# Expert tiles begun from the counts of eight token tiles, the rest of the router placed between them

## The chip, the cores and the metric

One NeuronCore of a Trainium2 chip runs the kernel. The metric is the device time of one execution in microseconds (us), as the median of several runs. Five engines work side by side, each with an instruction queue of its own: TensorE (PE in the profile, its weight loads PEld), VectorE (DVE), ScalarE (ACT), GpSimd (POOL) and SyncE (SP), which here issues nearly all DMAs. They wait for each other on semaphores. A lower time is better.

## The reference, cut to what matters

A small vision tower: 32 images of 36 patches, 192 channels, that is 1152 tokens. Patch embedding and a three-step "diffuser" attention come first; then a transformer block whose second half is a mixture of 8 experts with 2 chosen for each token:

```python
x = x + _attention(_layer_norm(x, ln1_g, ln1_b), ...)        # 12 heads of 16
xn = _layer_norm(x, ln2_g, ln2_b).reshape(B * N, C)
logits = xn @ gate_w                                          # 8 experts
top_logits, top_idx = jax.lax.top_k(logits, 2)
gates = softmax(top_logits)                                   # at top_idx, else 0
h = gelu(einsum('td,edh->teh', xn, w1) + b1)                  # hidden 768
y = einsum('teh,ehd->ted', h, w2) + b2
x = x + einsum('ted,te->td', y, gates)
```

and a last layer norm of the sum. Inputs have fixed shapes; which expert a token goes to depends on the data.

## The kernel before

**Tiling.** Tokens are worked on in NT = 11 tiles of T = 108 (three images); the last holds 72. The order of attention is `ATT` = tiles 8, 9, 10, 0 to 7, so an index `a` from 0 to 10 counts places in that order. The diffuser's steps come first, then a loop over `i` that runs attention for the tile `i` and, staggered behind it, later steps for the tiles `i - 1`, `i - 2` and `i - 3`: softmax and mixing of heads and projection for `i - 1` (L625 to 714), layer norm and transpose for the router for `i - 2` (L701), logits, choice of two experts, ranks and destination for `i - 3`. The loop runs to NT + 4 (L615, L1217, L1410), so its last iterations hold only the staggered steps of the last tiles. Each engine has this order written out by hand in its own block; within an engine it is strict.

**Router.** `logits(a)` (L586) is a matmul with the gate. `choose(a)` (L1189, VectorE) takes the best two of 8 and makes a 0/1 matrix `chosen`. `ranks(a)` (L593) are two matmuls with triangular and full ones, which give each row's rank within its tile and the tile's total for each expert. `send_to(a)` (L1205) adds the totals so far, `taken`, and gives each row two destinations. `send(a)` (L1402, GpSimd) writes the rows there with two indirect DMAs: `srt_dram` holds, for each expert, a region of rows in order of arrival.

**Table.** When all tiles are counted, VectorE works out the table of expert tiles (L1268 to L1299): the counts are rounded up to tiles of P = 128 rows, NTILE = 25 at most; for each tile its expert (packed seven to an integer, `packs`, semaphore `exp_ready`), the first row of it (`row_i`, `place_ready`), how many rows are valid, and then the softmax gates of all tokens, with an exponential on ScalarE (L988).

**Expert tiles.** SP waits for the table, reads expert and row into registers and loads the tile's `w1` weights (`expert_weights`, L370, three buffers) and its rows (`sorted_rows`, L378, a ring of 8). TensorE transposes the rows (`columns_of`, L724), ScalarE applies gain and bias (L990), VectorE casts to a high half `xh`, GpSimd subtracts to a low part `xl`; `first(i)` (L732) multiplies with `w1` in three terms, ScalarE applies gelu (L1000 to L1004), VectorE casts the hidden values to a high half and subtracts to a low part (`split`, L1305), and `second(i - 1)` (L749) multiplies with `w2`. VectorE adds `b2` (L1339), and GpSimd scatters the rows to `y_dram` (L1440). GpSimd also makes one of 22 diagonal gate matrices a tile (L1435). Some buffers of the tiles lie on those of earlier stages: the third `w1` buffer on the attention's weights, the rows' ring on the attention's buffers. At the end the two results of each token are loaded, weighted and added, and normalised.

## Time and profile before

| | |
|---|---|
| median of 3 runs | 416.79 us (415.52 to 416.88) |
| profiled execution, whole time | 420.47 us |
| its span, first to last instruction | 418.7 us |
| TensorE busy | 368.3 us (88%) |
| VectorE busy | 243.0 us (58%) |
| GpSimd busy | 216.7 us (52%) |
| ScalarE busy | 203.4 us (49%) |
| mean granted TensorE clock | 0.936 of full |

The profile is of one execution. All points in time below are us from the start of its span. Its page cuts the span into 40 slices of 10.5 us; further views group the work by stretch of time, list it in order of time, or follow the chain of work that ended last back from the end. A group's idle time before it, in square brackets, names who released it. The profiled execution's time is 3.7 us over the median of the runs.

In this trace the attention iteration `i` = 10, the last with attention scores, begins at 257.76, and the first expert matmul runs at 295.17.

### The profile page before, as it was taken

Reading aid. Unit: us, or ns where it says so; the run is one execution under the profiler, and the core shown is the slowest. Engines: PE = TensorE matmul, PEld = TensorE weight load, DVE = VectorE, ACT = ScalarE, POOL = GpSimd, SP = SyncE. Lnnn points to the kernel's source line nnn. Section 1 sums busy time; section 2 is a strip of 40 time slices with the busy share of each in tenths; the row PEclk is TensorE's granted clock in tenths of the full one; section 3 lists DMA queues with packets and bytes.
Section 4 is the critical chain, followed back from the end, with each engine's and each line's share of the span. In section 5 each row is a group of like instructions: output and inputs, shape, how many; then the busy total and the mean of one; then the engine's idle time right before and its main releaser. Section 6 shows DMA issues by size and latency. Waiting matters only on the chain.

```text
span 418.7 us, 11108 instructions
## 1 busy us (share of the span) xinstructions
PE 368.3 (88%) x3714; PEld 315.0 (75%) x3714; DVE 243.0 (58%) x721; ACT 203.4 (49%) x519; POOL 216.7 (52%) x361
## 2 busy tenths in 40 slices
PE   4999978999999988999989999760899999999963
PEld 3888745766766756898988999750899999899953
DVE  2111462454654565577876566546489888888622
ACT  1222276777577753657655455320554454454203
POOL 2001168666777652355777455452356667666324
PEclk9999999999999998999997799855699999999988
DMA  8999457966427422100000000024677666675052
GB/s 251 386 386 298 130 178 174 238 144 148 89 43 161 98 33 34 25 1 2 18 19 11 18 18 18 25 65 163 256 267 266 225 252 241 235 258 211 6 176 79
DMA packets 59558, 59.08 MB, mean 141 GB/s; under 512 B 36939, under 2 KB 46197, under 8 KB 58736
## 3 DMA queue, kind: packets, MB, share of 16 engines
q1 hardware_dynamic: 57248, 54.81, 43.1%
q0 software_dynamic: 2256, 3.57, 2.7%
q8 instruction: 32, 0.52, 0.5%
q14 instruction: 22, 0.18, 0.1%
HBM read 25.11 MB, written 14.33 MB: 94 GB/s over the span
## 4 chain that ended last, share of the span: by engine, by line
PE 77%; DVE 9%; issue 5%; ACT 3%; DMA 2%; POOL 2%; SPq 1%; ACTq 0%; POOLq 0%; DVEq 0%
PE bank L414 37%; PE wide L414 33%; PE bank L419 4%; PE bank L729 1%; DMA xT<-in_xT 1%; DVE xT L1160 1%; DVE stats L1037 1%; PE bank L632 1%; POOL rstd L1368 1%; DVE xs L1123 1%; ACT xT L966 1%; DMA xT<-y_dram 1%; ACT xT L800 1%; DMA y_dram<-ysb,ydst 0%; DMA xT<-srt_dram 0%
## 5 line engine op out<-in xcount | busy, mean ns | idle before, releaser
L1440 POOL DMA_INDIRECT y_dram<-ysb,ydst x25 | 25.8, 1032 | 36.1 <-DVE ydst L1321 27.5
L1367 POOL TENSOR_SCALAR veps<-mv 108x1 f32<-108x1 f32 x46 | 10.4, 225 | 61.1 <-DVE mv L1039 59.5
L414 PE MATMUL wide<-w2h,xs 128*128 x300 | 39.1, 246 | 0.0
L414 PE MATMUL bank<-wqv,xTs 128*108 128x384 f32 x96 | 37.4, 514 | 1.1 <-DVE xT L1160 1.0
L414 PE MATMUL wide<-w2l,xs 128*128 x150 | 36.9, 246 | 0.0
L1315 DVE TENSOR_TENSOR xs<-xT,xs 128x384 bf16<-128x384 f32 x50 | 35.6, 711 | 1.7
L831 ACT ACTIVATE xT<-bank,gains 96x128 f32<-96x128 f32 x50 | 20.0, 448 | 32.5 <-PE bank L729 32.5
L1313 DVE CAST xs<-xT 128x384 f16<-128x384 f32 x50 | 28.7, 575 | 11.2 <-ACT xT L1004 10.3
L800 ACT ACTIVATE xT<-bank 108x192 f32<-108x192 f32 (+3 forms) x57 | 20.9, 367 | 29.4 <-PE bank L414 16.2
L414 PE MATMUL bank<-tokw,xT 128*108 128x192 f32 x132 | 27.3, 364 | 6.2 <-DMA xT<-in_xT 5.2
L414 PE MATMUL wide<-xT 64*108 64x36 f32 (+2 forms) x368 | 30.7, 273 | 1.9 <-DVE chosen L1203 1.4
L414 PEld LDWEIGHTS wide<-xT 64*108 64x108 f32 (+1 forms) x368 | 28.3, 175 | 4.0 <-issue 3.6
L414 PEld LDWEIGHTS bank<-tokw,xT 128*108 128x108 f32 x132 | 24.2, 196 | 7.2 <-DMA tokw<-in_tokw 5.2
L414 PE MATMUL bank<-xTs,wqk 128*128 128x108 f32 x176 | 26.6, 297 | 3.2 <-DVE xT L1171 1.9
L1368 POOL TENSOR_TENSOR rstd<-veps,nhalf 108x1 f32<-108x1 f32 x46 | 26.2, 570 | 3.8
L1427 POOL TENSOR_TENSOR xl<-xT,xh 96x256 bf16<-96x256 f32 x25 | 21.0, 839 | 13.3 <-DVE xh L1303 12.7
L414 PEld LDWEIGHTS bank<-xT 108*32 108x32 f32 (+2 forms) x316 | 13.3, 119 | 18.0 <-issue 17.2
L1407 POOL DMA_INDIRECT srt_dram<-row,dst x22 | 23.0, 1044 | 7.1 <-issue 6.0
L414 PEld LDWEIGHTS bank<-xTs,wqk 128*128 128x128 f32 x176 | 23.1, 204 | 4.4 <-ACT xTs L831 2.2
L414 PEld LDWEIGHTS wide<-w2h,xs 128*128 128x128 f16 (+1 forms) x300 | 26.4, 98 | 0.0
L1131 DVE TENSOR_TENSOR rm<-bank,pairm 96x192 f32<-96x192 f32 x24 | 8.5, 353 | 30.8 <-PE bank L414 30.7
L1389 POOL TENSOR_SCALAR nrm<-nrm 108x4 f32<-108x4 f32 (+1 forms) x3 | 0.8, 274 | 47.3 <-DVE nrm L1094 33.0
(241 smaller groups left out, 1089.9 us busy)
## 6 DMA issues: line engine op xcount, KB each, us to landing
srt_dram<-row SPq DMA_DIRECT2D x8, 800.2 KB, 15.3
xT<-in_xT SPq DMA_DIRECT2D x11, 324.0 KB
tokw<-w1h SPq DMA_DIRECT2D x9, 384.0 KB
e1T<-w1l SPq DMA_DIRECT2D x9, 384.0 KB
xT<-in_w SPq DMA_DIRECT2D x8, 384.0 KB, 3.5
hT<-in_w SPq DMA_DIRECT2D x8, 384.0 KB, 3.3
vecs<-w1h SPq DMA_DIRECT2D x8, 384.0 KB
wqv<-w1l SPq DMA_DIRECT2D x8, 384.0 KB
```

The costliest lines, as they stand in the source:

```text
L414: return nc.tensor.matmul(o, l, r, start=start, stop=stop)
L419: last = nc.tensor.transpose(o[:, f, :], i[:, f * HF:(f + 1) * HF], ident[0:T, 0:T])
L800: return nc.scalar.activation(o, i, ACT.Copy)
L831: last = nc.scalar.activation(o[:, f], i[:, f], ACT.Identity, scale=gains[:, which, 0, f:f + 1], bias=gains[:, which, 1, f:f + 1])
L1131: V.tensor_tensor(rm[0:HF, q % 2], bank[3][0:HF, 0:2 * JB * PAIR].rearrange("p (u j c) -> p u j c", u=2, j=JB), pairm[0:HF, None, None, :] ...
L1313: V.tensor_copy(high, hidf[:, i % 2, cols]).then_inc(S["hidh_ready"], 1)
L1315: V.tensor_tensor(hidl[:, i % 2, o].rearrange("p j n -> p (j n)"), hidf[:, i % 2, cols], high, ALU.subtract).then_inc(S["hidl_ready"], 1)
L1367: link(G.tensor_scalar(ve, var, EPS, None, ALU.add))
L1368: last = G.tensor_tensor(rstd[0:rows, k], ve, nhalf[0:rows], ALU.pow)
L1407: G.indirect_dma_start(srt_dram, bass.IndirectOffsetOnAxis(dst[:, t, k:k + 1], 0), row[:, t, 0:W], None, bounds_check=EXP * CAP - 1, oob_i ...
L1427: G.tensor_tensor(xl[0:HF, i % 2], x32[:, i % 2], xh[0:HF, i % 2], ALU.subtract).then_inc(S["xl_ready"], 1)
L1440: G.indirect_dma_start(y_dram, bass.IndirectOffsetOnAxis(ydst[:, q:q + 1], 0), ysb[:, q % YB], None, bounds_check=2 * NTOK - 1, oob_is_err ...
```

## The change

The number of tokens that eight of the eleven token tiles bring (`SOON` = 8, the tiles `a` = 0 to 7, 828 tokens) guarantees that at least `FULL` = 5 expert tiles can be filled with 128 valid rows, whatever the router chooses. The change makes the table twice: a first one of 5 full tiles, with counts rounded down, in VectorE's iteration 10, ahead of the residual of tile 9; and a second one, of the other 20 tiles, after the last tile is counted, which is now in iteration 2 of the expert tiles. SP starts the first tiles from the first table and the stored rows of eight token tiles (`row_stored`), and waits for the second table (`exp_ready` 2, `place_ready` 2, `row_stored2`) before tile 5.

The router's steps move. Within an attention iteration the transpose for the router stands ahead of the values, its columns and the logits follow in the same iteration `i` for the tile `i - 2`; choice, ranks, destination and stores of the tile `i - 3` come at the start of the next. The loop ends at NT. What is left of the last tiles is written out around and between the first expert tiles: on TensorE the last probabilities, mixing, `columns_of(0)`, the last head columns, a router transpose, ranks, the last projection, `columns_of(1)`, `first(0)`, logits; then in tile 1 a transpose, ranks, and logits behind `second(0)`, and in tile 2 the last ranks.

Further edits: ring of 4 rows for 8; the router's columns are double-buffered instead of kept; `b2` is loaded earlier; the third weights' buffer waits for the last projection; for tiles below 5 the high cast of the hidden values is done by ScalarE instead of VectorE and no validity is looked up; the gelu table is loaded by a dummy activation ahead of tile 0; the gates' exponential comes after tile 5's gelus, and the gate diagonals in tiles 7 to 17, two a tile.

```diff
-RING, YB = 8, 3
+RING, YB = 4, 3
+SOON = NT - 3
+FULL = (2 * sum(min(T, B * N - t * T) for t in ATT[:SOON]) - EXP * (P - 1)) // P
+NPACK = 1 + -(-(NTILE - FULL) // PACK)
...
# SyncE
-            sp.wait_ge(S["row_stored"], 16 * 2 * NT)
+            sp.wait_ge(S["row_stored"], 16 * 2 * SOON)
...
             for i in range(WB, NTILE):
+                if i == FULL:
+                    sp.wait_ge(S["exp_ready"], 2)
+                    expert_weights(i)
+                    sp.wait_ge(S["place_ready"], 2)
+                    sp.wait_ge(S["row_stored2"], 16 * 2 * (NT - SOON))
                 sorted_rows(i)
-                expert_weights(i)
+                if i != FULL:
+                    expert_weights(i)
...
# TensorE, behind the attention loop (now range(NT))
+            probabilities(NT - 1)
+            mixed(NT - 1)
+            pe.wait_ge(S["taken_ready"], SOON)
             columns_of(0)
+            head_columns(NT - 1)
+            pe.wait_ge(S["xn_ready"], NT - 1)
+            turn(halves(3), row[:, ATT[NT - 2], 0:C]).then_inc(S["xnT_psum"], 1)
+            pe.wait_ge(S["e_ready"], NT)
+            ranks(NT - 3)
+            projected(NT - 1)
+            columns_of(1)
             pe.wait_ge(S["exp_ready"], 1)
...
+            first(0)
+            logits(NT - 2)
+            for i in range(1, NTILE + 1):
...
+                if i == 1:
+                    pe.wait_ge(S["xn_ready"], NT)
+                    pe.wait_ge(S["srtT_ready"], 2)
+                    turn(halves(1), row[:, ATT[NT - 1], 0:C]).then_inc(S["xnT_psum"], 1)
+                    ranks(NT - 2)
+                if i == 2:
+                    ranks(NT - 1)
+                    pe.wait_ge(S["taken_ready"], NT)
+                second(i - 1, e[(i - 1) % 2])
+                if i == 1:
+                    pe.wait_ge(S["taken_ready"], NT - 1)
+                    logits(NT - 1)
...
# ScalarE, expert tiles
+            nc.scalar.activation(vv[:, 1, 0:1], rowm[:, 0:1], ACT.Gelu)
...
+                gelus(i, (0, 2))
+                if i < FULL:
+                    high_of(i, 0)
+                if i == 1:
+                    router_columns(NT - 1, bank[1][0:HF, 0:2 * T].rearrange("p (f t) -> p f t", f=2))
+                gelus(i, (4,))
+                if i < FULL:
+                    high_of(i, 1)
+                if i == 0:
+                    router_rows(NT - 1)
+                if i == 5:
+                    act.wait_ge(S["gex_in"], 1)
+                    nc.scalar.activation(vv[:, 1, :], vv[:, 0, :], ACT.Exp).then_inc(S["gex_ready"], 1)
...
# VectorE, attention loop
+                if i == SOON + 2:
+                    table_tiles(0, FULL, eoff, 0)
+                    table_experts(0, FULL)
+                    table_places(0, FULL, eoff)
...
+                if i >= 1:
+                    residual(i - 1)
...
# VectorE, expert tiles
+            heads_of(NT - 1)
+            choose(NT - 3)
             sorted_high(0)
+            send_to(NT - 3)
+            residual(NT - 1)
             for i in range(NTILE + 1):
...
+                if i == 2:
+                    send_to(NT - 1)
                 if i < NTILE:
...
+                    if i == 0:
+                        choose(NT - 2)
+                    split(i, 0)
+                    if i == 1:
+                        send_to(NT - 2)
+                    split(i, 1)
...
+                if i == 1:
+                    choose(NT - 1)
+                if i == 2:
+                    table_tiles(FULL, NTILE, start[:], P - 1)
+                    sorted_high(4)
+                    table_experts(FULL, NTILE)
+                    table_places(FULL, NTILE, start[:])
+                if i == 3:
+                    table_valid(FULL, NTILE, start[:])
...
# GpSimd
+            sorted_low(0)
+            sorted_low(1)
+            residual(NT - 1)
+            send(NT - 3)
+            for i in range(1, NTILE + 1):
...
+                if i <= 2:
+                    send(NT - 3 + i)
+                if i == 7:
+                    pool.wait_ge(S["gates_ready"], 1)
```

`table_tiles`, `table_experts`, `table_places` and `table_valid` hold the instructions of L1269 to L1294, each over its own range of tiles and counted from a given start; `high_of` is the cast of L1313 as a ScalarE copy.

## Rows read from the trace of the kernel before

**Rows 1.** The page's 40 equal slices, busy tenths of TensorE and its granted clock.
```profile
PE   4999978999999988999989999760899999999963
PEclk9999999999999998999997799855699999999988
```
**Rows 2.** Stretches: length, busy time (and count) by engine, clock, DMA share, GB/s.
```profile
249.30:257.76 8.46, 8.40 (x85) 7.94 (x85) 5.58 (x21) 4.40 (x13) 3.74 (x6) 1.00 0.07 21
...
265.96:281.20 15.24, 9.79 (x57) 8.87 (x56) 8.27 (x42) 3.68 (x9) 8.14 (x13) 0.62 0.10 27
281.20:291.95 10.75, 0.93 (x4) 0.86 (x5) 6.68 (x31) 0.21 (x1) 3.40 (x4) 0.50 0.52 182
291.95:311.24 19.29, 17.16 (x210) 16.02 (x210) 11.21 (x30) 9.77 (x23) 7.50 (x10) 0.78 0.69 247
311.24:350.00 38.76, 37.77 (x554) 35.79 (x552) 33.53 (x80) 19.38 (x50) 25.59 (x30) 1.00 0.70 250
```
**Rows 3.** Chain that ended last, from residual to first expert matmul: start, us, what.
```profile
274.53 0.37 DVE xT L1260
...
286.00 0.30 DVE packs L1286
...
289.84 1.98 DMA xT<-srt_dram
291.95 0.65 PE bank L729 x2
...
295.17 2.72 PE bank L414 x24
```
**Rows 4.** Short stretches around changes of the granted clock, columns as rows 2.
```profile
225.00:225.50 0.50, 0.50 (x7) 0.50 (x6) 0.47 (x2) 0.18 (x1) 0.50 (x1) 0.68 0.17 47
235.00:235.50 0.50, 0.50 (x4) 0.47 (x2) 0.00 (x0) 0.50 (x2) 0.00 (x0) 0.58 0.14 37
269.00:270.00 1.00, 0.00 (x0) 0.00 (x0) 0.93 (x4) 0.00 (x0) 0.77 (x1) 0.78 0.00 0
300.00:301.00 1.00, 1.00 (x19) 1.00 (x17) 0.95 (x4) 0.75 (x3) 0.14 (x1) 0.86 0.41 160
```
**Rows 5.** Timeline of the attention's end: start, us, engine, line, out<-in, [idle before <-releaser].
```profile
264.28 0.61 DVE L1246 TENSOR_TENSOR xT<-wide,nmax 108x432 f32<-108x432 f32 x1
...
267.36 1.23 PE L414 MATMUL wide<-xT 108*108 108x147 f32 x8 [0.36 <-ACT xT L800]
...
269.49 0.76 DVE L1237 TENSOR_TENSOR xT<-wide,precm 108x576 f32<-108x576 f32 x1
270.30 2.13 PE L414 MATMUL bank<-amask,xT 108*96 108x36 f32 x12 [1.71 <-DVE xT L1237]
...
272.88 1.62 PE L414 MATMUL wide<-wvo,xT 128*108 128x192 f32 x4
274.28 0.83 PE L414 MATMUL wide<-chosen,rank 108*108 108x8 f32 x4
```
**Rows 6.** Timeline of VectorE: last choice, first to last; last placing; the table's first.
```profile
279.99 0.17 DVE L1197 MAX8 best<-wide 108x8 f32<-108x8 f32 x1 [0.33 <-PE wide L414]
...
280.89 0.17 DVE L1203 TENSOR_TENSOR chosen<-mm 108x8 f32<-108x8 f32 x1
...
282.17 0.17 DVE L1209 TENSOR_TENSOR pos<-wide,taken 108x8 f32<-108x8 f32 x1 [1.11 <-PE wide L414]
...
282.93 0.16 DVE L1269 SCALAR_TENSOR_TENSOR tiles_i<-taken,route 128x8 int32<-128x8 f32 x1
```
**Rows 7.** Chain again: the transposes of tiles 5 and 6's rows.
```profile
311.24 0.22 PE bank L729 x2
...
315.13 0.22 PE bank L729 x2
```
**Rows 8.** Timeline of ScalarE: the table load ahead of the first gelu.
```profile
295.06 1.28 ACT L1004 ACT_TABLE_LOAD   x1
```
**Rows 9.** Waits from 198 to 250: who for whom, us in total, times, longest.
```profile
PE wide L414 <- DVE chosen L1203: 1.4, 3, 0.6
```

## What the change does to the time: the prediction

> **What bounds the kernel now.** I read the busy slices of the page first. TensorE is 9 tenths busy or more in nearly every slice, with one hole: slices 26 to 28, where it falls to 6, 0 and 8 tenths while the granted clock reads 5, 5 and 6 tenths [rows 1]. The table of stretches puts times to it. The last full attention iteration (249.30 to 257.76, 8.46 us) has TensorE busy for 8.40 us. After the last iteration's own work (265.96) come 15.24 us with 9.79 busy at a mean clock of 0.62, then 10.75 us with 0.93 busy, then 19.29 us for the first five expert tiles with a mean clock of 0.78; from 311.24 on TensorE is busy 37.77 of 38.76 us [rows 2]. The chain of waits says what fills the hole: residual of the last token tile (274.53), router, counts, the table's experts on VectorE (286.00, 0.30 us, so published at 286.30), the sorted rows' load (289.84, 1.98 us), the transpose of the rows (291.95), and the first expert matmul at 295.17 [rows 3]. So from 265.96 to 295.17, 29.2 us, TensorE does little but a serial tail, and the last 9 us of it start from the finished table. That hole is what the change goes for; the expert tiles behind it are TensorE-bound at 3.89 us each (transposes at 311.24 and 315.13) [rows 7].
>
> The clock matters here. It fell to its lower level (half, 1.2 GHz) within 269 to 270 after TensorE had idled from 268.6, and came back within 300 to 301, some 5 us after matmuls ran densely again. It also fell within 225.0 to 225.5 with thin gaps before it and came back only within 235.0 to 235.5 although TensorE was busy all the time: 10 us [rows 4]. So after a restart I count 5 to 10 us at half clock.
>
> **First table, made early.** Eight token tiles' counts are ready in iteration 10, behind the scores' subtraction of that iteration (264.28 + 0.61 = 264.9) [rows 5]. Before, the table's first instruction started at 282.93 and the experts were out at 286.30, 3.4 us with 25 tiles a row [rows 3, 6]; with 5 tiles its wide instructions shrink, which I put at 0.8 us in all (0 to 1.2): experts at 267.5, places 0.8 us later, the new counts' start 0.4 us more: 268.7. From published experts to the first transpose took 291.95 - 286.30 = 5.65 us on SP and the DMA queue; the same steps give 273.1. The rows of the eighth tile must be stored by then: two indirect DMAs, given their addresses at about 262, have until the load is issued at 271, 9 us, where before the last two had from 283.0 to 289.84, 6.8 us [rows 3, 6].
>
> The cost is a delay behind it: VectorE adds the residual of token tile 9 at 268.7 instead of 266.0, so the last tile's heads (1.0 us for residual and moments, then 1.3) are done at about 271.1 instead of 270.25 (269.49 + 0.76) [rows 5]. On TensorE the last head columns are now queued behind the transpose of the expert rows, so they start at 273.7, not 270.30. TensorE idles from 268.6 (end of the matmuls of 267.36 in [rows 5]) to 273.1, so it restarts at half clock. In order: transpose 0.6, head columns 2.13, row transpose 0.6, ranks 0.83, projection 1.62, second expert transpose 0.6, all at half clock rates [rows 3, 5], sum 6.4: first expert matmul at 279.5. Before it was 295.17. **Tiles begin 15.7 us earlier.**
>
> **Router steps inside tiles 0 to 2.** Choosing takes 1.07 us (279.99 to 281.06) and placing 0.86 us (282.17 to 283.03) on VectorE, pauses included [rows 6]. The chain to the second table: tile 0's first product 3.9 us at half clock (the 2.72 us of 24 matmuls in [rows 3] scaled to 36) to 283.4; logits of token tile 9 0.9; its choice 1.1 (285.3), with tile 0's splitting behind it, 1.2 (286.6). Tile 1's first product (2.0) is over by then; a transpose and ranks 0.6, tile 0's second product 1.5: 288.6; logits of tile 10 0.5. VectorE meanwhile does split, placing of tile 9, split, bias, and then the last choice, over at 290.6. Tile 2's first product ends at 291.2, ranks 0.4, placing 0.9: 292.6. VectorE must still split tile 2 (1.5) and add tile 1's bias (0.4, after the second product at 293.5): 294.5. Then six table instructions for 20 tiles 1.5, a cast 0.3, six more 1.5: **second experts at 297.8**. Add the same 5.65 us: the transpose of tile 5's rows at **303.5**. TensorE is ready for it at about 297.3 and has the first product of tile 4 and the second of tile 3 queued behind it, so it idles about 6 us. In the kernel before this transpose is at 311.24 [rows 7]. So of 15.7 us won, 7.7 are left at tile 5: the second table's chain takes the hole over.
>
> After such an idle stretch the clock will be at half again for at least 5 us, in which some 2.5 us of work is lost, all behind 311.24's counterpart (before, that loss lies ahead of it, in the first tiles). Left: 5.2 us. If the clock comes back 5 us after 273.1 and not 10, the work of 278 to 283 is faster, and the chain ends 2.4 us sooner: 7.6 us. I take the middle, **6.4 us**.
>
> **Other edits.** (a) Expert weights: tile 2's wait for the last projection (278.9), needed by 289; 10 us of cover. (b) A ring of 4 rows for 8: the weights' loads between them already wait for the tile three back, so nothing. (c) The high cast on ScalarE for five tiles, ten casts of about 0.5 us: ScalarE is busy 19.38 of 38.76 us in steady tiles, VectorE 33.53 [rows 2]; this pays for about half of VectorE's 11 us of choosing, placing and table. VectorE's whole work from 268.7 to the fifth bias is some 26.5 us, until 295.2, under 303.5, so it is no bound of its own. (d) Diagonals moved to tiles 7 and on, two at a time: GpSimd busy 25.59 of 38.76 with one of them, about 0.7 us more per 3.9 us tile, still under. (e) The gates' exponential now sits between two gelus. The trace shows one table load, 1.28 us [rows 8]; two of them and the exponential's 0.2 give 2.8 us, against 1.9 us a tile in which ScalarE is free [rows 2, 7]: between 0 and 0.9 us for TensorE, taken as 0, since the products read the gelus a tile later. The same function's table for the first tile is now loaded ahead of the tiles, a gain that lies in the tail's cover.
> (f) Attention iterations: the choice leaves the path of the scores, where TensorE waited for it three times, 1.4 us in all [rows 9]; against this the head columns' copy stands behind the router columns on ScalarE (0.75 us) where TensorE already waits for it, and GpSimd issues the stores, some 2.4 us, ahead of its roots. Bounds: 2 us won (the three gaps and their echo), 2 us lost (0.75 in two or three iterations); taken as 0.
>
> The Trainium skill, "ScalarE: Activation LUTs", section "What ACT_TABLE_LOAD costs", speaks against (e): it adds a drain of some 1.38 us to each switch of tables. In the trace the load of 295.06 follows directly on the activation that ended at 295.04, with no drain to be seen. By that page the two switches would be an estimated 2.8 us dearer, so ScalarE would be 3.7 us late at tile 6 instead of 0.9, and the result up to 2.8 us later: 413.2.
>
> **Sum.** Span 418.7 - 6.4 = 412.3 us; the profiled execution took 420.47, 1.8 around the span: 414.1. The median of the runs shown, 416.79, is 3.7 under that execution; the half clock of 225 to 235 costs 5 us and may be missing in them, so I claim nothing for its going. 416.79 - 6.4 = **410.4 us**.
>
> **Rivals.**
> A. *The second table's wait is small.* If the clock stays up in the tail or comes back at once, and the load overlaps more, what is left is 15.7 less the added work on TensorE (about 2) and the waits between choice and ranks (about 1): up to 13, down to 9: 403.8 to 407.8. For: chains here are of small steps, and TensorE's are the halvable ones. Against: VectorE's steps and the 5.65 us of loading don't shrink. Chance 0.22, at 406.
> B. *The hole moves whole.* VectorE's queue in tiles 0 to 2 holds the last placing back by 3 to 6 us more (a cast beside GpSimd's work, its value loads, GpSimd's stores before the second load): 413.4 to 416.6. Chance 0.18, at 415.
> C. *Slower: the clock stays at half through tiles 0 to 4.* The 10 us of [rows 4] show that busy is not enough. Then two first and two second products in the chain take 7.0 us more, the transpose of tile 5 comes at 310.5, and with 2.5 us at half clock behind it the sum is -1.8: 418.6. It decides from a transpose of tile 5 later than 308.7. Chance 0.09.
> D. *It does not do what it says:* the early load waits for the stores of rows or for the weights' room until the tail is over, so tile 0 isn't early. The added router work remains: 417.5. Chance 0.04.
> Forecast as above, 408 to 413: chance 0.47.
>
> **How the numbers follow.** Range 403.8 (end of A) to 416.6 (end of B), leaving C, D and a strip beyond A. A difference under 0.3%, 1.25 us, can't be told from none here: faster is below 415.5. That is the forecast, A and three quarters of B, 0.82; same is the rest of B and a part of D, 0.06; slower C and most of D, 0.12.
>
> **What would show it.** Right: the first transpose of expert rows near 273, the first expert product near 279.5, a TensorE gap of about 6 us before tile 5's transpose near 303.5, clock at half around both, the same 3.89 us tiles and the same end. Wrong: no gap before tile 5 (A); a first table later than 270; attention iterations longer than 8.5 us late in the stage; the clock never at full between 270 and 303 (C).

## The result

The change doesn't make the kernel faster. In the first measurement the median of 20 runs was 423.75 us beside 422.24 for 20 runs of before. The recorded ratio is 1.0131 [1.0094, 1.0168]; it is that of the fast runs alone, 421.84 in the mean of twelve of the changed kernel over 416.40 in the mean of the first three of before, where the two medians above are only 0.4% apart. Timed twice more beside other kernels, it came out at 0.9993 [0.9936, 1.0050] and 0.9999 [0.9939, 1.0059]. So it is between 1.3% slower and equal; compared at the same mean clock (last section) it is 1.0% slower. The forecast, 410.4 us, 1.5% faster, is excluded by all three, and 423.75 lies outside the range.

The profiled execution took 421.68 us, with a span of 419.9 (before: 418.7). The slices of its page, TensorE and its granted clock, to be compared with [rows 1]:

```profile
PE   4999968999999987999988999797688999999873
PEclk9999999999999999977999989859889999999968
```

The slice in which TensorE stood still is gone; shallow ones took its place (7 tenths in slices 26 and 28, 6 in slice 29). The clock is down in slices 18 and 19, in the attention stage, earlier than before. Stretches of the same execution, columns as [rows 2]: last attention iteration, from there to the first transpose of expert rows, the tail up to the first expert products, tiles 0 to 4, tile 5, the next nine.

```profile
248.47:259.11 10.64, 10.07 (x85) 9.46 (x85) 5.72 (x21) 4.45 (x12) 3.75 (x6) 0.84 0.06 18
259.11:273.77 14.66, 10.74 (x94) 9.84 (x95) 11.58 (x50) 4.87 (x12) 5.42 (x10) 0.84 0.20 72
273.77:279.30 5.53, 5.53 (x30) 5.28 (x31) 1.60 (x8) 3.56 (x8) 0.67 (x1) 0.50 0.53 183
279.30:306.49 27.19, 18.98 (x221) 17.69 (x219) 15.20 (x65) 12.37 (x31) 13.81 (x17) 0.87 0.45 158
306.49:311.87 5.38, 5.38 (x56) 5.37 (x57) 1.22 (x4) 3.00 (x7) 0.66 (x1) 0.68 0.52 183
311.87:346.00 34.13, 31.73 (x469) 30.37 (x467) 28.15 (x70) 18.64 (x45) 22.65 (x28) 1.00 0.67 242
```

And the chain of work that ended last (start, us, what), to be compared with [rows 3, 7]:

```profile
263.47 0.76 DVE xT L1369
270.49 0.68 SPq L392
271.66 1.98 DMA xT<-srt_dram
273.77 0.63 PE bank L757 x2
...
279.10 2.56 PE bank L433 x24
...
292.31 1.97 another core or an unknown queue
295.00 2.02 PE wide L433 x18
303.20 0.67 SPq L392
304.38 2.06 DMA xT<-srt_dram
306.96 2.56 PE bank L433 x24
```

The first rows' load and transpose come 18 us earlier than in [rows 3] (273.77 for 291.95), and a second load, of tile 5's rows, now stands in the chain (304.38). Its transpose at 306.49 is the counterpart of 311.24 in [rows 7].

Stage by stage, from the timelines. A is the start of attention iteration 1 to that of iteration 10, B from there to the first transpose of expert rows, C from that to tile 5's, D from tile 5's to tile 10's, E from tile 10's to the end of the span, all in us:

| kernel | A | B | C | D | E | span |
|---|---|---|---|---|---|---|
| before | 85.4 | 34.2 | 19.1 | 19.5 | 88.1 | 418.7 |
| after | 90.5 | 14.7 | 32.7 | 22.6 | 90.8 | 419.9 |
| after, third time | 84.4 | 14.7 | 32.2 | 24.1 | 89.9 | 415.7 |
| old placing | 84.1 | 16.0 | 32.5 | 23.7 | 89.4 | 416.7 |
| high cast on VectorE | 91.2 | 14.7 | 31.9 | 22.5 | 89.3 | 422.7 |
| gates on GpSimd | 88.4 | 14.4 | 32.0 | 21.2 | 89.8 | 417.1 |
| old placing, short tail | 84.7 | 16.5 | 23.7 | 20.8 | 89.6 | 406.0 |
| the same, gates on GpSimd | 84.4 | 16.3 | 25.0 | 19.6 | 88.1 | 404.3 |

(The kernels below the third line are the experiments. C and D are cut at the first matmul of tile 5's transpose, for before 311.1, not the 311.24 of [rows 7].) In the first pair, B and C together win 19.5 - 13.6 = 5.9 us, and A loses 5.1, D 3.1 and E 2.7. That is 5.0 us lost from iteration 1 on. After's iteration 1 began 3.8 us earlier (168.62 against 172.38), which is the stage ahead of it, hardly touched by the change; hence the 1.2 us between the spans. In the fourteen traces of this document that start lies anywhere from 168.6 to 176.9, so a single pair of spans says little.

### The profile page after: what moved, and what is told of

Read it like the earlier page. It is cut to its first block, busy times and chain, and to the rows that moved or that the text cites. A ratio compares the mean times of both kernels' runs of the same rounds, so it can differ in the third digit from the quotient of the medians.

```text
span 419.9 us, 11160 instructions
## 1 busy us (share of the span) xinstructions
PE 369.0 (88%) x3714; PEld 315.7 (75%) x3714; DVE 240.1 (57%) x724; ACT 210.7 (50%) x532; POOL 215.8 (51%) x361
## 4 chain that ended last, share of the span: by engine, by line
PE 71%; DVE 9%; issue 5%; DMA 4%; ACT 4%; POOL 3%; SPq 2%; another core or an unknown queue 0%; DVEq 0%; ACTq 0%; POOLq 0%
PE bank L433 35%; PE wide L433 30%; PE bank L438 4%; PE bank L757 1%; DVE xT L1260 1%; DMA xT<-in_w 1%; DMA xT<-y_dram 1%; DMA xT<-srt_dram 1%; POOL rstd L1533 1%; DMA xT<-in_xT 1%; ACT xTs L892 1%; PE bank L639 1%; DVE xs L1223 1%; DVE stats L1137 1%; SPq L389 1%
## 5 line engine op out<-in xcount | busy, mean ns | idle before, releaser
L1448 DVE TENSOR_TENSOR xs<-xT,xs 128x384 bf16<-128x384 f32 x50 | 33.6, 677 | 6.3 <-ACT xs L861 4.7
L433 PE MATMUL bank<-wqv,xTs 128*108 128x384 f32 x96 | 35.5, 492 | 1.8 <-DVE xT L1260 1.5
L861 ACT ACTIVATE xT<-bank 108x192 f32<-108x192 f32 (+3 forms) x57 | 21.0, 369 | 29.4 <-PE bank L639 19.6
L433 PE MATMUL wide<-xT 64*108 64x36 f32 (+2 forms) x368 | 32.6, 280 | 0.7 <-ACT xT L861 0.6
L433 PEld LDWEIGHTS wide<-xT 64*108 64x108 f32 (+1 forms) x368 | 29.6, 178 | 3.1 <-issue 2.0
L433 PE MATMUL bank<-tokw,xT 128*108 128x192 f32 x132 | 25.6, 347 | 6.2 <-DMA xT<-in_xT 5.2
L433 PEld LDWEIGHTS bank<-xTs,wqk 128*128 128x128 f32 x176 | 24.5, 214 | 7.0 <-ACT xTs L892 4.8
L433 PEld LDWEIGHTS bank<-tokw,xT 128*108 128x108 f32 x132 | 22.7, 184 | 7.1 <-DMA tokw<-in_tokw 5.2
L1446 DVE CAST xs<-xT 128x384 f16<-128x384 f32 x40 | 23.9, 598 | 6.3 <-ACT xT L1070 4.1
L433 PEld LDWEIGHTS bank<-xT 108*32 108x32 f32 (+2 forms) x316 | 13.0, 117 | 18.1 <-issue 16.8
L1596 POOL TENSOR_TENSOR xl<-xT,xh 96x256 bf16<-96x256 f32 x25 | 20.9, 838 | 11.0 <-DVE xh L1433 10.4
L1554 POOL TENSOR_SCALAR nrm<-nrm 108x4 f32<-108x4 f32 (+1 forms) x3 | 0.8, 276 | 45.6 <-DVE nrm L1194 31.3
```

What stands on the lines that cost most here:

```text
L433: return nc.tensor.matmul(o, l, r, start=start, stop=stop)
L861: return nc.scalar.activation(o, i, ACT.Copy)
L1446: V.tensor_copy(high, hidf[:, i % 2, cols]).then_inc(S["hidh_ready"], 1)
L1448: V.tensor_tensor(hidl[:, i % 2, o].rearrange("p j n -> p (j n)"), hidf[:, i % 2, cols], high, ALU.subtract).then_inc(S["hidl_ready"], 1)
L1596: G.tensor_tensor(xl[0:HF, i % 2], x32[:, i % 2], xh[0:HF, i % 2], ALU.subtract).then_inc(S["xl_ready"], 1)
```

## The experiments

**The changed kernel again.** First: is the loss in A there each time? Nothing was edited.

> The changed kernel, nothing altered, beside the kernels below on the same chip. From the first profile: slower than before by about 1.3%, 5 us; from the start of attention iteration 1 to that of iteration 10 about 90.5 us (before 85.4); first expert transpose 14.7 us after the start of iteration 10; a TensorE gap of about 2.5 us ahead of the second product of tile 1, one of about 4.3 us ahead of tile 5's transpose, one of about 2.2 us in tile 8. If the 5 us of the attention stage are the placing of the work and no accident of one execution, they are here again (88 to 92). Rival: they are the dip of the clock in one execution, then this trace shows 85 to 87 and the total is within 0.3% of before.

A took 92.7 us (some 21 of its first 50 us at half clock) and the span 427.0 at a mean granted clock of 0.914; the ratio was 0.9993. B was 14.7, and the gap ahead of tile 5's transpose and that in tile 2 were there again. The stages repeated, and the rival's "same total" came true as well, so total and stages had to be taken apart.

**The old placing of the router steps in iterations 0 to 9** (early table kept; the ranks' sums also go to another bank of PSUM, the matmuls' output memory).

```diff
 # TensorE, iteration i; iteration 10 keeps one step more
-features(i, 1); ranks(i - 3)
+logits(i - 3); features(i, 1)
...
-turn(halves2, row[i - 2]); values(i); head_columns(i - 1); to_columns(i + 1)
-logits(i - 2); projected(i - 1)
+values(i); head_columns(i - 1); to_columns(i + 1); turn(halves2, row[i - 2])
+projected(i - 1); ranks(i - 3)
 # ScalarE: router_columns(i - 2) last; VectorE: choose behind qbd, send_to last; GpSimd: send last
```

> The changed kernel, but token tiles' router steps of attention iterations 0 to 9 placed as before: logits behind the probabilities' transposes, ranks last in the iteration, the turned rows behind the columns of the next tile, ScalarE's router columns last, placing behind the residual on VectorE, GpSimd's stores behind its roots. Iteration 10 has one step more (logits, choice, ranks of the eighth tile and the turn and logits of the ninth), and the early table as in the changed kernel. Theory 1 (the spreading of the router steps is what costs the attention stage 5 us, since the transposes' and ranks' matmuls no longer cover the way head columns, copy, exponential, next columns): iterations 1 to 10 take 85 to 87 us, and the whole is 3 to 5 us faster than the changed kernel, about even with before (-2 to +1 us). Iteration 10 gets 0.5 to 1 us longer. Theory 2 (the extra time there comes from the clock or from GpSimd's and SP's queues): iterations 1 to 10 still take 89 us or more and the total is within 1 us of the changed kernel.

A took 84.1 us (after: 90.5), B 16.0 (after: 14.7), the total 417.95 against 421.87 in the medians of runs timed together, 0.9873 [0.9745, 1.0002] of before. The sizes are near those of theory 1 (A was forecast at 85 to 87), but the interval just holds 1, and A's gain contains the clock, as the next traces show.

> The changed kernel with the old placing in attention iterations 0 to 9, once more: 0.7 to 1.5% under the changed kernel, 0 to 0.8% under before, iterations 1 to 10 in 84 to 86 us. If the placing of the router steps costs nothing: within 0.3% of the changed kernel.

> The changed kernel, nothing altered: 0.5 to 1.5% slower than before, iterations 1 to 10 in 90 to 92 us, clock down within 182 to 186 us of the span, 11 to 13 us after iteration 1 began. If its first result was an accident of the chip: within 0.3% of before.

The second time, A of the old placing was 85.4, the ratio to before 0.9983 [0.9941, 1.0024], medians 417.73 and, for the changed kernel, 420.88; that is 0.75% apart, as expected. But the third profile of the changed kernel had A at 84.4, and its total was 0.9999 of before: its three expectations (0.5 to 1.5% slower, A 90 to 92, clock down at 182 to 186) failed, and "within 0.3% of before" came true. The windows say why A was short: its clock stayed up all through A. So did that of one kernel below that has the old placing ("Stores ahead of the scatter"). These two are the clean pair, columns as [rows 2]; first the changed kernel:

```profile
170.43:254.84 84.41, 78.44 (x767) 72.59 (x767) 63.04 (x208) 50.06 (x131) 55.41 (x133) 1.00 0.08 25
```

and the old placing:

```profile
171.55:253.05 81.50, 76.98 (x763) 72.81 (x763) 60.99 (x203) 49.15 (x130) 53.92 (x131) 1.00 0.08 24
```

At full clock throughout, A is 84.41 - 81.50 = **2.9 us** longer with the router steps spread. Half of it is standing time (5.97 us idle for 4.52), half is busy time (78.44 for 76.98). Of the busy half, one more call of the logits is a part, four matmuls and 0.46 us, which the old placing does in iteration 10; the rest of that half isn't explained. And B is 16.0 and 16.1 us in the two traces of the old placing with the changed tail, for 14.4 to 15.2 with the steps spread, so about 1.3 us come back there: up to the first expert transpose, spreading costs some 1.6 us against the old placing. TensorE's waits in iterations 2 to 9 (the group that waited, its releaser, us in total, times, longest), changed kernel, third time:

```profile
PE wide L433 <- ACT xT L861: 2.2, 5, 0.6
PE bank L433 <- ACT xTs L892: 1.7, 8, 0.2
PE bank L433 <- DVE chosen L1303: 1.3, 3, 0.6
PE bank L438 <- ACT row L976: 0.7, 1, 0.7
```

and old placing:

```profile
PE wide L434 <- ACT xT L870: 2.0, 4, 0.7
PE wide L434 <- DVE chosen L1313: 1.4, 3, 0.7
PE bank L434 <- ACT xTs L901: 0.4, 2, 0.2
```

(The old placing has one more, of 0.6 us, for which the profile names no releaser.) The wait for the next tile's columns (xTs) comes in eight iterations and not two; the wait for the normalised router rows (row) is new. The choice, which the change wanted off the path, is waited for as long as before, 1.3 for 1.4 us, only by another instruction.

**Ranks alone put back** to the end of iterations 3 to 9, the rest of the spreading kept.

```diff
-    ranks(i - 3)          # behind features(i, 1)
...
     logits(i - 2)
     projected(i - 1)
+    ranks(i - 3)          # likewise send_to on VectorE, send on GpSimd
```

> The changed kernel, but of the spread router steps only the ranks' matmuls (with placing and stores) go back to the end of attention iterations 3 to 9; the turned rows, router columns and logits stay as changed. Of the 5 to 6 us that the spreading costs from iteration 1 to 10, theory 1 (ranks were the cover for the columns of the next tile on TensorE) gives back 1.5 to 2.5 us: 88 us, and the waits of 0.2 us ahead of the features are gone, those ahead of the last projection (0.36 to 0.55) stay. Rival (all of it is ScalarE's order, the router columns ahead of the head columns' copy): it stays at 90 to 91 us.

One execution was measured, 423.23 us, too few for a verdict. A was 88.6, with other stretches of half clock in it, so only undisturbed iterations compare: 7, 8 and 9 took 8.16, 8.28 and 8.47 us, those of the changed kernel the third time 9.05, 9.11 and 8.99, and the old placing 9.06, 8.74 and 8.40. TensorE's waits from 240.56 to 265.47, these three iterations (PEld is its weight load):

```profile
PEld wide L433 <- DVE xT L1396: 0.8, 3, 0.5
PE wide L433 <- DVE xT L1396: 0.2, 1, 0.2
```

Both waits for ScalarE are gone, not only that for the columns as theory 1 had it. In the late iterations the ranks' early place is the whole cost: 8.30 us on average without it, 9.05 with it (and 8.73 with everything in its old place). They were what TensorE did last, while ScalarE made the next tile's columns. Iteration 4, undisturbed in the three traces too, took 9.55 us with the ranks late, 10.21 in the changed kernel and 9.27 with the old placing; there the ranks are 0.66 of 0.94 us, and the rest belongs to the other moved steps.

**Where the clock falls.** In A the clock fell once in before (225 to 236) and in the changed kernel twice (183 to 195, and at 248 for some 3.4 us). What TensorE did just before the first of these, in the timeline of iteration 2:

```profile
182.89 0.39 PE L438 MATMUL bank<-ident,row 108*96 108x108 f32 x2 [0.98 <-ACT row L976]
```

and the windows at both ends:

```profile
183.00:184.00 1.00, 1.00 (x9) 1.00 (x9) 0.93 (x4) 1.00 (x3) 0.00 (x0) 0.93 0.00 0
184.00:185.00 1.00, 1.00 (x8) 1.00 (x8) 0.14 (x1) 1.00 (x4) 0.69 (x2) 0.50 0.00 0
194.00:195.00 1.00, 1.00 (x9) 1.00 (x10) 0.50 (x4) 1.00 (x3) 0.00 (x0) 0.95 0.00 0
```

The wait for router rows is 0.97 or 0.98 us long in six of the seven traces that have it. In these six the clock falls 0.9 to 1.5 us behind it and stays down for 6.8 us (three of them) or 10.2 us (the other three). In the seventh, the third of the changed kernel, it is

```profile
184.38 0.39 PE L438 MATMUL bank<-ident,row 108*96 108x108 f32 x2 [0.67 <-ACT row L976]
```

and the clock stays at its upper level (2.4 GHz). That speaks for this gap as the trigger, but no experiment took it away alone, and the falls elsewhere speak against its length as the measure. Before the fall at 213.9 in the second trace of the changed kernel, and before that at 225.2 in the kernel before, the only wait of the last 3 us was

```profile
211.01 0.55 PE L433 MATMUL bank<-chosen,rank 108*108 108x8 f32 x4 [0.49 <-DVE chosen L1303]
222.61 1.33 PE L414 MATMUL wide<-xT 64*108 64x36 f32 x24 [0.65 <-DVE chosen L1203]
```

So falls followed gaps of 0.49 and 0.65 us where 0.67 was followed by none, and the trigger isn't shown. What the traces do show is that the clock falls somewhere in A in twelve of fourteen: in six of the seven with the old placing, for 6.8 or 10.2 us in all, and in six of the seven with spread router steps, for 10.2 to some 21 us. The arithmetic closes, though: iterations 2 and 3 took 12.22 and 11.21 us at half clock against 9.77 and 9.29 without, 4.4 us, and iteration 9 10.64 against 8.99, 1.7 us; 90.5 - 84.4 = 6.1. In before the same sum is 3.6 us (iterations 6 and 7, 10.57 and 11.59, against 9.51 and 9.06 of the old placing at full clock). So of the 5.1 us in A of the first pair, 2.6 to 2.9 are placing and the rest is clock.

**The high cast back on VectorE** (term (c)).

```diff
-                if i < FULL:
-                    high_of(i, 0)        # and (i, 1), on ScalarE
...
-                if i >= FULL:
+                if True:
                     V.tensor_copy(high, hidf[:, i % 2, cols]).then_inc(S["hidh_ready"], 1)
```

> The changed kernel, but the high halves of the hidden values of the first five tiles are cast on VectorE as in the other tiles, ten casts of some 0.5 us taken back from ScalarE. Theory (VectorE's queue of choosing, placing and splitting sets when the second table is done): second table 3 to 5 us later, the gap ahead of tile 5's transpose wider by as much, total 3 to 5 us slower than the changed kernel. Rival (the chain to the second table waits on TensorE's logits and ranks, VectorE has room between): second table later by under 1.5 us, total within 1.5 us.

The rival was right about the stage: C 31.9 us for 32.7, second experts 26.8 us after the first transpose for 27.4, both within what the unedited kernel shows from trace to trace (C 30.9 to 32.7). The total, 424.64 us in the median of four runs for 421.87, is too noisy to bear on it. The casts on ScalarE buy nothing; VectorE waits on the chain between its steps.

**The gates' exponential on GpSimd** (term (e)). In the changed kernel ScalarE does this in the middle of tile 6:

```profile
315.29 1.28 ACT L1104 ACT_TABLE_LOAD   x1
316.58 0.21 ACT L1104 ACTIVATE vv<-vv 108x11 f32<-108x11 f32 x1
316.70 0.79 ACT L892 ACTIVATE xT<-bank,gains 96x128 f32<-96x128 f32 x2
317.51 1.28 ACT L1070 ACT_TABLE_LOAD   x1
318.80 0.66 ACT L1070 ACTIVATE xT<-wide 128x256 f32<-128x256 f32 x2
```

and TensorE at tile 8:

```profile
325.56 0.22 PE L433 MATMUL bank<-xh,wqk 128*128 128x128 f16 x1 [2.17 <-issue]
```

```diff
+euler = sb("euler", [T, 1])                    # set to e on GpSimd
-    nc.scalar.activation(vv[:, 1, :], vv[:, 0, :], ACT.Exp).then_inc(S["gex_ready"], 1)
+    G.tensor_tensor(vv[:, 1, :], euler.broadcast_to([T, NT]), vv[:, 0, :], ALU.pow).then_inc(S["gex_ready"], 1)
```

> The changed kernel, but the gates' exponential between the activations of tiles 5 and 6 is taken from ScalarE and made on GpSimd (a power with a constant base), so that ScalarE loads no table inside the expert tiles. Theory (the two table loads of 1.28 us delay a gelu, the splits behind it and then the rows of tile 8): the TensorE gap of 2.2 us in tile 8 is gone, tiles 6 to 10 take 15.6 us as before and not 17.2, total 1.5 to 2.2 us faster than the changed kernel. Rival (the gap comes from the register load on VectorE and the scatter ahead of the low part on GpSimd, not from the table loads): the gap stays above 1.5 us, total within 0.5 us.

The gap fell from 2.17 to

```profile
323.81 0.22 PE L434 MATMUL bank<-xh,wqk 128*128 128x128 f16 x1 [0.74 <-issue]
```

although the power took GpSimd 2.27 us; from tile 6's transpose to tile 10's it took 15.9 us for 17.2 (before: 15.6). So the switch costs 1.3 us in this pair. Over all traces that stretch is 16.7 to 18.8 us in the nine with the switch and 15.8 to 16.3 in the four without, so about 1 us is the safer figure; in the longest, of 18.8, a half-clock stretch of some 3.4 us followed the gap. The total, 425.03 against 421.87 in four and ten runs, doesn't show a gain: the noise is larger.

**The tail in another order,** on top of the old placing. The idea: the second table waits for two choices that stand behind tiles' products in TensorE's queue.

```diff
 probabilities(NT - 1); mixed(NT - 1)
-columns_of(0); head_columns(NT - 1); turn(halves(3), row[NT - 2]); ranks(NT - 3); projected(NT - 1)
-columns_of(1); first(0); logits(NT - 2)
-columns_of(2); first(1); turn(halves(1), row[NT - 1]); ranks(NT - 2); second(0); logits(NT - 1)
-columns_of(3); first(2); ranks(NT - 1); second(1)
+head_columns(NT - 1); turn(halves(3), row[NT - 2]); ranks(NT - 3); columns_of(0); logits(NT - 2); projected(NT - 1)
+columns_of(1); first(0); ranks(NT - 2)
+columns_of(2); turn(halves(1), row[NT - 1]); first(1); logits(NT - 1); second(0); ranks(NT - 1)
+columns_of(3); first(2); second(1)
 # ScalarE, VectorE and GpSimd follow; the second table is made at the end of tile 1, not of tile 2
```

> The kernel with the old placing in attention iterations 0 to 9, and now another order in the tail and tiles 0 and 1: head columns and the turned rows of the tenth token tile ahead of the first expert transpose, its logits ahead of the first product of tile 0, its ranks right behind that; the last token tile's turn, logits and ranks in tile 1, and the second table on VectorE at the end of tile 1, not of tile 2. Theory (the hole ahead of tile 5 is the chain of the last two token tiles' choices, most of it queueing behind tiles' products, so that it can be had earlier): second experts some 8 to 10 us earlier than in the kernel with the old placing alone (there 26.5 us after the first expert transpose began, then 17 to 19), first transpose to tile 5's transpose 23 to 26 us and not 32.5, no half clock behind it; total 6 to 9 us faster than the kernel with the old placing alone, 410 to 412. Rival (the time goes to GpSimd's stores and the loading of rows, or to the clock at half for longer since TensorE restarts earlier): the transpose of tile 5 comes less than 4 us earlier and the total gains under 3 us.

Second experts stood 17.8 us after the first transpose and not 27.3, C was 23.7 us and not 32.5, and the total 407.31 us beside 416.34 of before: 0.978 [0.9618, 0.9943]. The first transpose itself came 0.5 us later, since the head columns now stand ahead of it. With the gates on GpSimd added, and that kernel once more on another chip:

> As the kernel with the old placing and the shorter tail, and with the gates' exponential made on GpSimd, so that no table is loaded inside the tiles. Theory: the gap in tile 8 is gone, tiles 6 to 10 in 15.6 to 16 us; 1 to 1.5 us faster than without this, 409 to 411 in all, some 2.5% faster than before. Rival: less than 0.5 us between the two.

> The kernel with old placing, shorter tail and the gates on GpSimd once more, beside the changed kernel and the one with the old placing alone on one chip. If the parts add up as the stages of the traces say: 2.0 to 2.8% under before, 3 to 3.8% under the changed kernel. If the chip of the first time was kind to it: less than 1.5% under before.

It took 405.38 us beside 416.34, 0.9799 [0.9709, 0.9889], and on the other chip 414.21 beside 419.68, 0.9894 [0.9823, 0.9964]. That is less than the expected 2.0 to 2.8%; the case named for a first chip that was kind, under 1.5%, came true. Tiles 6 to 10 took 15.8 us against 16.8 without the gates' edit. This fixed kernel (old placing, new tail, gates on GpSimd) is 1 to 2% faster than before, and 1.6% faster than the changed kernel in the medians of the other chip (414.21 for 420.88). What is left of the hole lies, in its first trace, between tile 4's and tile 5's transposes, where TensorE waits 2.14 us for GpSimd's low part of tile 3 and then 2.6 us for the rows of tile 5; GpSimd in that stretch:

```profile
285.93 1.01 POOL L1636 DMA_INDIRECT y_dram<-ysb,ydst  x1 [1.61 <-DVE dst L1325]
287.24 1.01 POOL L1583 DMA_INDIRECT srt_dram<-row,dst  x1 [0.30 <-issue]
288.55 0.99 POOL L1583 DMA_INDIRECT srt_dram<-row,dst  x1 [0.30 <-issue]
289.57 0.67 POOL L1609 TENSOR_TENSOR xl<-xT,xh 96x256 bf16<-96x256 f32 x1
```

**Stores ahead of the scatter.**

```diff
-                if i >= 1:
-                    q = i - 1
+                for q in () if i == 1 else (0, 1) if i == 2 else (i - 1,):
...
-                    link(V.tensor_reduce(start[:], ...))     # behind table_places(0, ...)
+            link(V.tensor_reduce(start[:], ...))             # behind choose(NT - 3)
```

> The kernel with old placing, shorter tail and the gates on GpSimd, and two more edits: GpSimd issues the stores of the last token tile's rows before the first scatter of results and not behind it (there the low part of tile 3 ended at 290.24 and TensorE waited 2.1 us for it, and 2.6 us for tile 5's rows, issued at 292.78); and the new counts' start is worked out behind the heads of the last token tile instead of ahead of its residual (0.5 us on VectorE). Theory: low part of tile 3 and the rows of tile 5 each 1.3 us earlier, first to tile 5's transpose 22.5 to 24 us and not 25.0, total 1 to 2.5 us faster: 403 to 404.5 where before is 416.3. Rival (something else queues: SP's weight loads or the landing of the stores): within 0.5 us.

The two waits did shrink, to 0.60 and 1.41 us, but C stayed at 24.6 (25.0): VectorE waited 1.23 us behind tile 1 for a signal that the profile can't name, and the second experts came 19.3 us after the first transpose, not 17.9. The second trace of the kernel without these two edits has the same wait, 1.24 us, with the second experts at 19.1 and C at 24.2, so the wait isn't the edits' doing. The total was 412.5 us beside 421.11, 0.9859 [0.9795, 0.9923], between the two ratios without the edits. The rival, no gain, stands.

**The wait without a name.** In tile 2 of the changed kernel VectorE and ScalarE, which both wait for TensorE, get their signals late. VectorE:

```profile
294.30 0.17 DVE L1309 TENSOR_TENSOR pos<-wide,taken 108x8 f32<-108x8 f32 x1 [1.99 <-remote]
```

TensorE, whose ranks it waits for, had started them at 291.96:

```profile
291.96 0.58 PE L433 MATMUL wide<-chosen,rank 108*108 108x8 f32 x4 [0.57 <-DVE chosen L1303]
295.00 0.34 PE L433 MATMUL wide<-w2h,xs 128*128 x2 [2.46 <-DVE taken L1310]
```

Their placing releases TensorE, so about 1.8 us of the gap of 2.46 are this. A load of instructions (0.02 MB, on the DMA queue of kind instruction) began at 290.2. Is it that?

```diff
+            for _ in range(64):
+                pe.wait_ge(S["pad_ready"], 1)      # ahead of TensorE's first matmul
```

> The changed kernel with 64 waits that are already fulfilled ahead of TensorE's first matmul (it waits there 5.2 us for data anyway): the same work, its instructions only lie elsewhere in memory. In the changed kernel ScalarE and VectorE both wait 1.3 to 2 us in tile 2 for TensorE's signals with nothing that the profile names, 3 to 4 us behind a load of instructions. Theory (TensorE stands still for its instructions there): the wait moves to another place or goes, first to tile 5's transpose 29.5 to 31 us and not 32.7. Rival (it is something in the order of the work): the wait is there again, in tile 2.

The wait was there again, in tile 2:

```profile
294.89 0.17 DVE L1312 TENSOR_TENSOR pos<-wide,taken 108x8 f32<-108x8 f32 x1 [2.67 <-remote]
```

C was 31.3 us and the one execution took 422.24: the rival. Whether the 64 waits moved the code far enough can't be seen. The wait, 1.2 to 2.7 us on VectorE, is in every trace of the changed tail but that with the ranks alone put back, where C is 29.0 us and not 31 to 33. Its cause stays open.

## Why the prediction was wrong

*First table.* Right. Predicted from the start of iteration 10 to the first transpose: 273.1 - 257.76 = 15.3 us, measured 14.7; from transpose to first product 6.4, measured 5.3 (279.10). The clock came back at 283, 9 us after the restart at 273.8, within the 5 to 10 us that the prediction counted.

*Second table's chain.* Right in kind, 2.3 us short. First transpose to tile 5's: 303.5 - 273.1 = 30.4 predicted, 32.7 measured (30.9 to 32.7 in eight of the nine traces with this tail). By steps: choice of tile 9 over at 12.2 us after the first transpose (predicted) and 10.6 (measured); choice of tile 10 at 17.5 and 18.1; its counts added at 19.5 and 20.9 (the wait without a name takes 1.8 of it); second experts 24.7 and 27.4; load and transpose 5.65 and 5.3. The other part is the step from counts to experts, 6.5 us for 5.2: tile 1's second product waits on TensorE for that placing, and the table on VectorE for that product's bias. It was over 2.4 us behind the counts (295.00 + 2.02, partly at half clock); the step had left some 1 us for it. That VectorE is no bound of its own was right (cast experiment).

*Clock behind the gap.* Right: half clock from 306 to 311, tile 5 took 5.4 us for 3.9, 1.5 lost where 2.5 were set; a second such stretch, 296 to 300, followed the gap in tile 2.

*(f), attention iterations, taken as 0 with bounds of 2 us either way.* **This is the step that failed.** It is 2.9 us at full clock, beyond the bound, and 5.1 in the first pair. The prediction weighed two waits: the choice, which it put at up to 2 us won, and the head columns' copy behind the router columns, 0.75 us "in two or three iterations". It did not ask what the moved ranks and turned rows had covered. [rows 9] told only of the wait that would go. The waits for ScalarE's columns, 0.2 us each in two iterations of before, became eight, because the ranks no longer stood ahead of them, and the choice was waited for just as long from its new place. And the prediction gave no price to the clock in A: a new wait of 0.98 us stands right before a half-clock stretch of 6.8 or 10.2 us in six of seven traces, though that the one causes the other isn't shown.

*(e), the gates' exponential, taken as 0 out of 0 to 0.9.* It is 1.3 us in the pair, about 1 over all traces: ScalarE 2.8 us late delays a gelu, that the split on VectorE, that the result's bias and a scatter on GpSimd, and the scatter stands ahead of the low part that tile 8 needs. "The products read the gelus a tile later" left out the third and fourth engine. By the Trainium skill, "ScalarE: Activation LUTs", section "What ACT_TABLE_LOAD costs", a drain of some 1.38 us would come to each switch. The trace disagrees, as it did before the change: the activation of 316.58 follows the load of 315.29 with no drain between, and the load itself stands 0.02 us behind the activation that ended at 315.27.

*(a) to (d).* No wait for weights' room shows in tiles 0 to 2, so (a) and (b) were nothing. (c) was nothing too, not half of VectorE's burden. (d) wasn't tried alone.

*The base.* The 416.79 us that the forecast starts from was the median of three runs of before; the 20 beside the changed kernel had 422.24. Of the 13.4 us between forecast and measured median, 5.5 are this, luck of the draw and no part of the mechanism. Taken off 422.24, the same 6.4 would give 415.8, still 7.9 us too low.

*The sum.* -18.9 + 11.1 + 1.4 (the gap's clock and the choice of a middle) = -6.4 was set. Measured from iteration 1: +5.1 (A) - 19.5 (B) + 13.6 (C) + 1.5 (tile 5) + 1.6 (tiles 6 to 9) = +2.3, and 2.7 more from tile 10 to the end. Of these last, up to 2 us are the final stage, 33.4 to 34.6 us from tile 24 in the traces of the changed kernel and its one-part variants against 32.5 in before and 32.2 to 32.9 in those with both gates and tail edited. That was neither predicted nor explained. Taken together: 2.9 for placing, 1.3 for the table switch and 2.3 for the longer chain are 6.5 us and use up the 6.4. That the three cancel so exactly is partly luck, as each is read from one or two traces; the clock in A and the end make what is left of the first measurement's 1.3%.

*The rivals.* D, that the early load waits for stores or weights' room, didn't come: tile 0 began 16 us earlier. B, the hole moves whole, was closest in kind: 416.6 at its end. Its reasons (VectorE's queue, GpSimd's stores) were not the ones, since its share in C was only 2.3 us. C, clock at half through tiles 0 to 4, gave the right sign for the wrong reason: the mean clock there was 0.87 in the first trace. The wrong sign had its way in through a stage that the prediction had set to nothing.

## What to carry to other kernels

When a step is moved, list what its old place covered, not only the wait that its move removes: TensorE's cheap steps at the end of an iteration were the time in which ScalarE made the next input. When a chain is started early so that two halves overlap, the second half's chain gets the queueing of the first half's work; ordering TensorE's queue by that chain, logits and ranks ahead of products, made stages B and C together 40.2 to 42.7 us here for 47.2 and 48.5, 5 to 8 us that starting early alone had not brought. And an edit "behind other work" has to be followed through every engine that waits in order, up to the one that bounds.

## What the runs showed of the hardware

Most of the scatter between runs goes with the granted clock. Over 58 runs of before (four chips) the mean granted clock went from 0.913 to 0.959 and the time from 428 to 410 us; a straight line through them falls 3.4 us for each 0.01 and leaves 1.3 us. Read off at 0.94, before is 418.0 us, the changed kernel (42 runs) 422.2, with the old placing (16) 419.5, and the fixed one (12 runs, ten of them above 0.94) 414 to 415. The clock is partly the kernel's own doing, so this isn't a verdict, but it orders the kernels as the stages do. A single pair of profiles doesn't: the changed kernel's three had spans of 419.9, 427.0 and 415.7.

A GpSimd power over 108x11 took 2.27 us beside VectorE's work, where ScalarE's exponential took 0.21 and two loads of 1.28; it was still the cheaper one here: TensorE's gap at tile 8 was 0.74 us with it and 2.17 without.
